# A Mamba-style mixer with a routed feed-forward on one core: 17 early expert blocks, a longer return ring, the output bias as one product, mixed blocks in 64 columns

## What is computed

```python
diff = x[:, :, None, :] - keys
logits = -sum(diff * diff, -1) + x @ rw.T + rb
topv, topi = top_k(logits, 4);  w = softmax(topv)
hidden = gelu(einsum("bld,efd->blef", x, w1) + b1)      # F = 512
exp_out = einsum("blef,edf->bled", hidden, w2) + b2     # b2: [16, 128]
x = layernorm(x + sum(w * take(exp_out, topi)))
```

## Time and profile before

| | us |
|---|---|
| median of 3 runs (381.27 to 386.13) | 385.67 |
| profiled execution, first to last instruction | 313.4 |
| PE busy in it | 273.5 (87%) |
| ACT, DVE, POOL busy | 214.7, 185.6, 152.1 |

### The profile page before, as it was taken

The page is one execution under the profiler, slowest core; times in us unless marked ns, Lnnn a source line. Parts: engine busy times, 40 slices in busy tenths (PEclk is TensorE's granted clock), DMA queues, the critical chain, the costliest instruction groups (busy, mean ns, idle before and its releaser), DMA issues.

```text
span 313.4 us, 11661 instructions
## 1 busy us (share of the span) xinstructions
PE 273.5 (87%) x3534; PEld 252.7 (81%) x3535; DVE 185.6 (59%) x817; ACT 214.7 (69%) x763; POOL 152.1 (49%) x167
## 2 busy tenths in 40 slices
PE   3989699988998757997996999999999999997591
PEld 3978577877787646997995999999999999995481
DVE  3135437877887865747876665566655566641272
ACT  1572538878787752784874688888888889884064
POOL 3103400037777677787677766555555564424000
PEclk9976679999999967799999799999999999999687
DMA  6999900001111212332232322222222222100973
GB/s 210 213 369 350 459 19 5 2 22 58 60 57 60 59 57 81 96 86 79 57 89 66 87 79 79 63 81 64 67 69 68 72 66 63 38 12 7 327 251 92
DMA packets 25408, 32.44 MB, mean 104 GB/s; under 512 B 4316, under 2 KB 18293, under 8 KB 25105
## 3 DMA queue, kind: packets, MB, share of 16 engines
q1 hardware_dynamic: 20576, 22.38, 24.2%
q0 software_dynamic: 4352, 8.79, 8.2%
q10 hardware_dynamic: 432, 0.67, 0.8%
HBM read 20.84 MB, written 11.50 MB: 103 GB/s over the span
## 4 chain that ended last, share of the span: by engine, by line
PE 74%; DVE 6%; ACT 6%; issue 6%; DMA 5%; SPq 1%; POOL 0%; ACTq 0%; POOLq 0%; DVEq 0%
PE bank L760 19%; PE bank L781 19%; PE bank L755 4%; PE bank L561 4%; PE bank L842 3%; PE bank L745 3%; ACT hs L1570 3%; PE bank L771 3%; PE bank L576 2%; PE bank L532 2%; PE bank L603 2%; PE bank L641 1%; DVE shared L962 1%; PE bank L548 1%; PE bank L845 1%
## 5 line engine op out<-in xcount | busy, mean ns | idle before, releaser
L1894 POOL DMA_INDIRECT yrows<-shared,idi x72 | 76.6, 1064 | 57.4 <-ACT shared L1752 33.3
L1826 POOL DMA_INDIRECT xrows<-rows_all,sli x64 | 62.1, 971 | 54.3 <-issue 50.7
L1733 ACT ACTIVATE shared<-bank,shared 128x128 f32<-128x128 f32 x256 | 72.9, 368 | 20.2 <-PE bank L760 19.8
L760 PE MATMUL bank<-shared 128*128 128x128 f32 x512 | 70.0, 281 | 6.0 <-issue 6.0
L760 PEld LDWEIGHTS bank<-shared 128*128 128x128 f32 x512 | 64.3, 197 | 7.3 <-issue 7.3
L781 PE MATMUL bank<-w2s,shared 128*128 x512 | 68.7, 278 | 0.1
L781 PEld LDWEIGHTS bank<-w2s,shared 128*128 128x128 f32 x512 | 63.1, 194 | 0.4 <-issue 0.3
L1383 DVE COPY shared<-w1s 128x644 f32 x64 | 33.0, 516 | 28.4 <-issue 27.3
L1752 ACT ACTIVATE shared<-shared,idg 128x128 f32<-128x128 f32 x72 | 30.0, 419 | 9.3 <-DVE shared L1396 7.9
L962 DVE TENSOR_TENSOR shared<-bank,small 128x512 f32<-128x512 f32 x32 | 21.2, 683 | 5.4 <-PE bank L576 5.2
L1719 ACT ACTIVATE shared<-bank 128x128 f32<-128x128 f32 x72 | 20.8, 289 | 4.5 <-PE bank L745 4.3
(11 more groups left out here) (233 smaller groups left out, 480.2 us busy)
## 6 DMA issues: line engine op xcount, KB each, us to landing
shared<-xrows SPq DMA_DIRECT2D x64, 70.0 KB
w1s<-in_w1T SPq DMA_DIRECT2D x1, 4128.0 KB, 23.0
w2s<-in_w2T SPq DMA_DIRECT2D x1, 4096.0 KB, 23.1
w1s<-yrows SPq DMA_DIRECT2D x8, 512.0 KB, 6.8
yrows<-shared,idi POOLq DMA_INDIRECT x72
xrows<-zrow SPq DMA_DIRECT2D x1, 1120.0 KB, 11.9
w1s<-in_b SPq DMA_DIRECT2D x1, 1024.0 KB, 22.4
xrows<-rows_all,sli POOLq DMA_INDIRECT x64, 2.4
```

Of the source, the lines that this page charges most:

```text
L760: m = mm(hidden_bank(u)[:, f * P:(f + 1) * P], w[:, f * P:(f + 1) * P], xbT[u][:, :], start=True, stop=True)
L1733: m = act(hT[u][:, f * P:(f + 1) * P], hidden_bank(u)[:, f * P:(f + 1) * P], ACT.Gelu, bias=w[:, F + f:F + f + 1])
L1826: po.indirect_dma_start(out=xrows, out_offset=bass.IndirectOffsetOnAxis(ap=sli[:, g, k:k + 1], axis=0), in_=rows_all[:, g, :], in_offset=N ...
L1894: po.indirect_dma_start(out=yrows, out_offset=bass.IndirectOffsetOnAxis(ap=idi[r][:, 0:1], axis=0), in_=yw[r][:, :], in_offset=None, bound ...
```

## The change

- `EARLY` is 4 and `NE` is 17. `early_table` and the product that feeds it come one stage sooner.
- Result buffers `yw` and row numbers `idi` are rings of 16 for the first 30 blocks and of 8 after them (`home`, `last_put`), where they were of four. The loop is unrolled by 8; the peeled steps before it are 0 to 31, as they were.
- POOL sends all pairs ahead of any return. `last_root` stands in the middle of pair 5's sends, `last_gates` behind them.
- The routing of pair 7 has a bank of its own (`late_of`), and the orders of PE, DVE and ACT in the mixer's drain are rewritten: on DVE `take_w1` of block 0 comes after `normed(6)`, that of block 1 after `slots(6)`, and `res_stats(7)`, `res_moments(7)` and `last_var` between blocks 1 and 2.
- The gate is multiplied on DVE straight from PSUM (`weigh`); `out_bias`, the copies `yb` and ACT's `weigh` go. `b2` is no longer repeated over partitions in `w1s`; instead DVE makes a table of gates by row and expert in six operations (`gate_rows`), PE turns it, and at the end one product of gates and `b2` for each group adds the bias. The copied weights are 516 columns wide, not 644.
- Mixed blocks: PE's hidden layer is made in 64 columns of weights at a time (32 matmuls for 16), the rows are turned by products of 64 columns; the second expert's w1 is loaded by SP from HBM (2 buffers) where DVE copied it, and its w2 is copied by DVE, not by ACT.

```diff
+RY, RE = 8, 16
+EARLY_HOMES = 4 * RY - 2
...
-EARLY = 5
+EARLY = 4
...
+def early_puts(home):
+    return len([b for b in range(EARLY_HOMES) if b % RE == home])
...
+    def home(self):
+        return self.off % (RE if self.early_ring() else RY)
+    def last_put(self):
+        if self.early_ring():
+            return 16 * (self.off // RE)
+        turns = early_puts(self.home()) + self.off // RY - (EARLY_HOMES + RY - 1 - self.home()) // RY
+        if self.peeled:
+            return 16 * turns
+        return self.base * (16 * (self.unroll // RY)) + 16 * turns
...
+        def late_of(m_):
+            return bank[6] if m_ == NP - 1 else late
...
-        N3, LO3 = NBLK + 2, (NE + 7) // 4 * 4
+        N3, LO3 = NBLK + 2, 4 * RY
...
             sp.dma_start(xrows.rearrange("(e r) w -> r e w", e=E)[0:P, :, :],
                          zrow[:].unsqueeze(1).broadcast_to([P, E, ROW])).then_inc(zero_out, 16)
-            sp.dma_start(w1s[:, :, 0:F + FB], d["w1T"]).then_inc(ld["w1"], 16)
-            sp.dma_start(w1s[:, :, F + FB:WB], d["b2"].partition_broadcast(P).rearrange("p (e f) -> p e f", e=E)
-                         ).then_inc(ld["b2"], 16)
+            sp.dma_start(w1s[:], d["w1T"]).then_inc(ld["w1"], 16)
             sp.dma_start(w2s[:], d["w2T"]).then_inc(ld["w2"], 16)
-            sp.wait_ge(tab_done, 1)
-            sp.wait_ge(s1["yi_mm"], NT - 2)
...
                 if b.mixed():
                     for h in range(2):
-                        r = sp.value_load(tbi[0:1, 1, bass.ds(b.entry(h), 1)], min_val=0, max_val=E * S - HB)
-                        sp.dma_start(xb[b.slot(RB)][h * HB:(h + 1) * HB, :], xrows[bass.ds(r, HB), :]
+                        sp.dma_start(xb[b.slot(RB)][h * HB:(h + 1) * HB, :], xrows[bass.ds(row_at(b.entry(h), HB), HB), :]
                                      ).then_inc(got[b.slot(RB)], 16)
+                    if b.off >= NF + 2:
+                        sp.wait_ge(s3["ht_act"], b.back(2).count())
+                    ex = expert_at(mybir.EngineType.SP, b.entry(1))
+                    sp.dma_start(w1d[b.slot(2)], d["w1T"][:, bass.ds(ex, 1), :].rearrange("p o f -> p (o f)")
+                                 ).then_inc(got_w[b.slot(2)], 16)
                     return
...
+            run_steps(sp, rows_in, NF, RY, LO3, NBLK)
...
+                if b.mixed():
+                    for h in range(2):
+                        m = mm(turned_rows()[h * HB:(h + 1) * HB, :], xb[b.slot(RB)][:, h * HB:(h + 1) * HB], ident,
+                               start=True, stop=True, skip_group_check=True)
+                    m.then_inc(s3["bt_mm"], 1)
...
                 if b.mixed():
+                    pe.wait_ge(got_w[b.slot(2)], 16 * ((b.off - NF) // 2 + 2))
                     for f in range(FB):
-                        for h, wh in enumerate((w, w1d[b.slot(RB)])):
-                            m = mm(hidden_bank(u)[:, f * P + h * HB:f * P + (h + 1) * HB], wh[:, f * P:(f + 1) * P],
-                                   xbT[u][:, h * HB:(h + 1) * HB], start=True, stop=True, skip_group_check=True)
+                        for h in range(2):
+                            for c_ in range(2):
+                                m = mm(hidden_bank(u)[c_ * HB:(c_ + 1) * HB, f * P + h * HB:f * P + (h + 1) * HB],
+                                       (w, w1d[u])[h][:, f * P + c_ * HB:f * P + (c_ + 1) * HB],
+                                       xbT[u][:, h * HB:(h + 1) * HB], start=True, stop=True, skip_group_check=True)
                     m.then_inc(s3["h_mm"], 1)
...
             pe.wait_ge(s1["sm1_dve"], NT)
-            rows_transpose(Step(0, 4, 0, True))
+            rows_transpose(Step(0, RY, 0, True))
             moe(0)
             positions(6)
-            rows_transpose(Step(0, 4, 2, True))
-            hidden(Step(0, 4, 1, True))
             y_transpose(7)
-            expert_out(Step(0, 4, 0, True))
+            rows_transpose(Step(0, RY, 2, True))
+            hidden(Step(0, RY, 1, True))
             out_product(7)
-            for b in range(2, 9):
+            expert_out(Step(0, RY, 0, True))
+            for b in range(2, 5):
                 moe(b)
             positions(7)
-            for b in range(9, 16):
+            for b in range(5, 11):
                 moe(b)
             blocks()
...
+            def gates_turned():
+                pe.wait_ge(g_dve, 6)
+                for h in range(2):
+                    m = pe.transpose(bank[6][:, h * P:(h + 1) * P], gd16[:, h * P:(h + 1) * P], ident)
+                m.then_inc(gt_mm, 1)
+            def step3_turned(s):
+                if s.peeled and s.off == LO3 - 1:
+                    gates_turned()
+                step3(s)
...
             for g in range(NG):
-                mm(bank[g][:, 0:GT * D].rearrange("p (t d) -> p t d", t=GT), ident,
-                   rows_all[:, g * GT:(g + 1) * GT, 0:D], start=True, stop=False)
+                to = bank[g][:, 0:GT * D].rearrange("p (t d) -> p t d", t=GT)
+                mm(to, ident, rows_all[:, g * GT:(g + 1) * GT, 0:D], start=True, stop=False)
+                k = g % 4 * GT * D
+                mm(to, gT[:, g // 4, :], b2d[:, k:k + GT * D].rearrange("p (t d) -> p t d", t=GT), start=False, stop=False)
...
             def row_ids(b):
                 r = b.slot(RB)
                 ve.wait_ge(s3["gt_dve"], b.count())
-                if b.had(RB):
-                    ve.wait_ge(put[r], b.back(RB).dma(RB))
+                if not b.early_ring() or b.last_put() > 0:
+                    ve.wait_ge(put[b.home()], b.last_put())
                 skip = pm[:, b.off - NF:b.off - NF + 1] if b.mixed() else pen[:, bass.ds(b.val(), 1)]
-                tt(idi[r][:], idg[r][:, 0:1], skip, ALU.add).then_inc(s3["id_dve"], 1)
+                tt(idi[b.home()][:], idg[r][:, 0:1], skip, ALU.add).then_inc(s3["id_dve"], 1)
+            def weigh(b):
+                ve.wait_ge(s3["yb_mm"], b.count())
+                if not b.early_ring() or b.last_put() > 0:
+                    ve.wait_ge(put[b.home()], b.last_put())
+                ts_(yw[b.home()][:], out_bank(b.slot(2)), idg[b.slot(RB)][:, 1:2], None, ALU.mult).then_inc(s3["yw_dve"], 1)
             def take_w1(b):
-                r = b.slot(RB)
                 if b.had(RB):
                     ve.wait_ge(s3["ht_act"], b.back(RB).count())
-                    ve.wait_ge(s3["yb_dve"], b.back(RB).count())
-                if b.mixed():
-                    for h, to in enumerate((w1c[r], w1d[r])):
-                        ex = expert_at(mybir.EngineType.DVE, b.entry(h))
-                        m = ve.tensor_copy(to[:], w1s[:, bass.ds(ex, 1), :].rearrange("p o f -> p (o f)"))
-                    m.then_inc(s3["w1_dve"], 1)
+                ex = expert_at(mybir.EngineType.DVE, b.entry(0) if b.mixed() else b.val())
+                ve.tensor_copy(w1c[b.slot(RB)], w1s[:, bass.ds(ex, 1), :].rearrange("p o f -> p (o f)")
+                               ).then_inc(s3["w1_dve"], 1)
+            def take_w2(b):
+                if not b.mixed():
                     return
-                ve.tensor_copy(w1c[r][:], w1s[:, bass.ds(expert_of(mybir.EngineType.DVE, b), 1), :].rearrange("p o f -> p (o f)")
-                               ).then_inc(s3["w1_dve"], 1)
-            def out_bias(b):
-                u = b.slot(2)
-                ve.wait_ge(s3["yb_mm"], b.count())
-                if b.had(2):
-                    ve.wait_ge(s3["yw_act"], b.back(2).count())
-                if b.mixed():
-                    for h, wh in enumerate((w1c[b.slot(RB)], w1d[b.slot(RB)])):
-                        r = slice(h * HB, (h + 1) * HB)
-                        m = tt(yb[u][r, :], out_bank(u)[r, :], wh[r, F + FB:WB], ALU.add)
-                    m.then_inc(s3["yb_dve"], 1)
-                    return
-                tt(yb[u][:], out_bank(u), w1c[b.slot(RB)][:, F + FB:WB], ALU.add).then_inc(s3["yb_dve"], 1)
+                if b.off >= NF + 2:
+                    ve.wait_ge(s3["yb_mm"], b.back(2).count())
+                ex = expert_at(mybir.EngineType.DVE, b.entry(1))
+                ve.tensor_copy(w2d[b.slot(2)][:].rearrange("p f d -> p (f d)"),
...
+            def gate_rows(k):
+                h, what = divmod(k, 3)
+                t = slice(h * NT // 2, (h + 1) * NT // 2)
+                if k == 0:
+                    ve.wait_ge(s1["pk_act"], NP - 2)
+                if k > 0:
+                    ve.wait_ge(g_dve, k)
+                if what == 0:
+                    m = tt(gq, c("eids").rearrange("p (k e) -> p k e", k=TOPK).unsqueeze(1).broadcast_to([P, NT // 2, TOPK, E]),
+                           rows_all[:, t, RA:RI].unsqueeze(3).broadcast_to([P, NT // 2, TOPK, E]), ALU.is_equal)
+                if what == 1:
+                    m = tt(gq, gq, rows_all[:, t, RG:ROW].unsqueeze(3).broadcast_to([P, NT // 2, TOPK, E]), ALU.mult)
+                if what == 2:
```

(97 more changed lines are left out.)

273 lines of the change are left out of this document (146 added, 127 removed).

## The result

| | before | after |
|---|---|---|
| median of 4 runs | 385.9 us (381.3 to 387.4) | 406.5 us (405.4 to 407.3) |
| ratio after/before, 95% interval | | 1.061 (1.055 to 1.066) |
| profiled execution: time, span | not given, 313.4 us | 406.8 us, 405.0 us |

Two later comparisons, each with its own runs of before, gave 1.043 (1.036 to 1.050) and 1.040 (1.034 to 1.046). So the loss is 16 to 21 us.

The account below looks back on a forecast made before the run. PE was taken to bound the kernel, full in the middle, held up before 180 us and in the tail. Terms -1.2 + 0.6 + 4.5 - 3.6 = +0.3 us on 385.67 gave 386.0 us, range 377 to 393.5 us.

Parts of the forecast that it names:

- 72.3 us above that span: Whole kernel: runs' median exceeds the 313.4 us profiled span by 72.3 us, which the change leaves alone; 385.67 + 0.3 = 386.0 us.
- Drain and sends: Mixer's drain to block 22: waits shrink, a late block 2 eats most of it; 1.2 us won against 179.46 us.
- The late block 2: First blocks: `take_w1` of block 2 stands behind `res_stats(7)`, so block 2 starts at 135.2 us, 4.2 us later than before.
- the wait for block 17's rows: Drain: later sends land block 17's rows at 166.6 us, PE wants them at 164.9; block 17 starts at 168.7 us.
- Mixed blocks: Tail of eight mixed blocks: SP's loads behind the gelu make steps 3.95 us instead of 3.02; 4.5 us lost.
- The chain behind the gelu: Mixed blocks: from the gelu through SP's weight and row loads until the rows land, 4.8 us in all.
- 1.2 us for the clock: Mixed blocks: PE, less busy, may run at a lower granted clock; 1.2 us added to the 3.3 us lost.
- the first two free: Mixed blocks: of the eight, the first two are not held by the loop over SP's loads, the others are.
- End: After the last output: first group waits 7.85 us against 8.3, groups take 18.2 instead of 21.9 us; 3.6 us won.
- Being busy, it should not sink in clock: End: PE, busy with residual and gates times `b2`, keeps its clock, so all eight groups run at 1.30 us.
- Gates: Steps 25 to 30: six `gate_rows` operations exceed DVE's slack and PE's turning waits for the sixth; 0.6 us lost.
- The one on row loads behind the weights: Rival, mixed blocks: row loads queue behind 264 KB of weights, steps cost 7 to 8 us more; 393.7 us, chance 0.12.

Follow-up runs that it names:

- before_again: The kernel before, unchanged, profiled once more: 386.5 us, with a span of 384.7 us.

## Why the prediction was wrong

**The step that failed** is "The median of the runs is 72.3 us above that span; I see nothing in the change that moves what lies around it". Nothing of that size lies around the span, 1.8 us do. The 72.3 us were inside the span of every timed run, as the hold-up, and the profile had come from an execution without it, like those on chip 11. The number was in front of me, and 19% of a kernel's time outside its span was a contradiction to be explained, not a constant to be carried along. Everything about the mixer and the drain was then read from an execution in which sends cost the other engines nothing.

**Drain and sends, -1.2 us forecast, +7 to +11 us measured.** What the order of instructions does came as written: `take_w1` of block 0 ended at 176.13 us, 4.3 us behind `y_scale(7)` (171.41 and 0.42 us); POOL idled 10.65 us ahead of the root (186.07 us, in the earlier trace rows at 139.50); the returns started behind the last send in one row. The late block 2, the 4.2 us that were to eat the gain, did not show: it came 11.3, 9.7 and 9.7 us after block 0 in three executions of after (forecast 9.4), but 9.8 us in before_again too, which I had not known. But the wait for block 17's rows never showed, since ACT and PE stood still between blocks 5 and 8 for 15 and 13 us. That the one row of transfers makes this stall is likely, not shown: breaking the row up moved the stall to the returns and left the total, and with all sends spaced in both kernels 8.7 us of the loss stood (79.7 against 71.0 us). For it speaks chip 11, where the same stretch with spaced sends and returns was 2.2 us shorter than before's.

**Mixed blocks, +4.5 us forecast, +7.8 us measured.** Mechanism right, size too small. The chain behind the gelu, forecast at 4.8 us, took 4.8 and 4.4. I had set 27.0 us from step 65 to the end of the last output against 23.1, taken 0.6 us off in step 64 and added 1.2 us for the clock; from the hidden layer of block 65 (347.19) to the end of the last output (378.53) it is 31.3 us. The term that was too small is "the first two free": on PE the rows of block 67 are turned ahead of the hidden layer of block 66, so the loop holds already there, and from the hidden layer of block 65 to that of block 66 go 5.76 us, the longest step of all. The five steps after it took 3.9 us on average, as forecast (3.95). The 1.2 us for the clock can't be told apart in this; the granted clock over the mixed part was 0.90. At the end the last output stood 1.88 us without an instruction, where before had a gap of 0.96 us. The Trainium skill's remark that packing leaves the emptying of PSUM as it is (TensorEngine Tiling (Array Packing), Performance Considerations) did not decide here: the sixteen pairs took 0.93 us as worked out from rows 7 (eight groups 0.116 us apart, from 344.80 us), and PE stood waiting for rows (7.4 us in three waits), not for ACT.

**End, -3.6 us forecast, -1.8 us measured.** The groups ran at the later pace of the earlier trace rows from the first, 1.03 and 0.59 us, as said. But PE's products of residual and gates took 8.65 us instead of 7.4 and started 0.6 us late: from 378 to 383 us the granted clock was 0.66, in the 5 us after that 1.00, and the first four rows took 0.94 to 1.19 us. "Being busy, it should not sink in clock" failed:

```profile
379.13 1.19 PE L907 MATMUL bank<-rows_all,cst 128*128 128x256 f32 x2 [0.60 <-issue]
380.12 1.06 PE L909 MATMUL bank<-b2d,gmx 128*128 128x256 f32 x2
...
387.35 0.59 PE L909 MATMUL bank<-b2d,gmx 128*128 128x256 f32 x2
387.78 1.03 PE L913 MATMUL bank<-w1s,cst 128*128 128x256 f32 x4
```

Added work ahead of a wait had become the bound: the loads were there, and PE was not.

**Gates, +0.6 us forecast, +0.7 us measured.** The step in which PE turns the gates takes 2.60 us instead of 1.90, in each of the three traces of after:

```profile
277.65 0.44 PE L889 MATMUL bank<-cst,gmx 128*128 128x128 f32 x2 [0.27 <-DVE gmx L1477]
```

The stretch in the table hides it, 81.8 against 81.6 us, because before_again has its stop of 1.6 us there. The last two full steps take 2.25 us each instead of 1.90; there PE already turns rows for mixed blocks in the new form.

No rival named what happened. The one on row loads behind the weights gave 393.7 us, by another cause.

## What to carry to other kernels

Compare the profiled span with the timed runs before reading anything else; if they differ by more than the few microseconds of a launch, the profile is of another condition, and no sum made in it holds for the time. Where one engine issues indirect transfers in a row, look at the others for "issue" gaps in loops without waits, and try a pause of some 0.7 us between transfers if they show; where they don't, the same pauses cost 10% here. A load put behind a wait in a queue delays everything queued behind it; count the loop that this closes from the first step in which the queue waits.

## What the runs showed of the hardware

- The same kernel takes 314 us on one chip (11) and 384 to 387 us on chips 1, 12 and 13 and in the first comparison, with the runs of each comparison within 2.5%. The difference is in the stretches where POOL issues indirect transfers 0.30 us apart: PE runs 59 to 72 matmuls in 10 us there, against 248 at the same place (88 to 98 us) in the profile of rows 1 to 10, with the same eight sends a pair, and ACT and DVE stop with it.
- Pauses of 0.30 and 0.42 us between the transfers leave the hold-up as it is, one of 0.71 us takes most of it away. Returns at 1.9 us from one to the next, in the middle blocks, never caused it.
- A long row can stop ACT for 15.2 and PE for 13.4 us with their inputs ready. What carries this from POOL to the others, instruction supply or the delivery of semaphores, isn't settled. The gaps inside PE's loops, at instructions without any wait, speak for the first. For the second speaks DVE, which stood 15.6 us until 218.48 for the output that PE had ended at 206.89 by its modelled end. Slow transfers of code don't show: the queues marked "instruction" carried nothing from 203.7 to 231.4 us, and one block of 16 KB took 0.9 to 1.6 us in the profile of before as in before_again and after. Why one chip is free of it stays open too.
